# Second-layer sums of a two-layer graph network: gather by tile into a shared ring instead of by step

## What is computed

```
edge_index = stack([src, dst])
x = layernorm(x + layer0(x, edge_index, edge_type_64, ...))

# layer 1
x0_i = leaky(x @ W1 + b1);  x0_j = leaky(x @ W2 + b2)      # slope 0.2
a1 = x0_i @ wa1 + ba1[0];   a2 = x0_j @ wa2 + ba2[0]       # one number per node
row, col = edge_index
att = sigmoid(a1[row] + a2[col])                           # one number per edge
out = segment_sum(att[:, None] * x0_j[col], row, num_segments=12500)
x = layernorm(x + (out + x))
```

## Time and profile before

| | us |
|---|---|
| median of three runs | 7085.9 (7082.45 to 7089.11) |
| span of the profiled execution, first to last instruction | 6353.0 |
| the profiled execution's own device time | not recorded |
| median of the runs less the span of the profile | 732.9 |
| busy: PE / DVE / ACT / POOL | 4654.9 / 4416.1 / 2770.5 / 4352.2 |
| first gather of `attend` starts / last one starts | 4151.36 / 6255.98 |

### The profile page before, as it was taken

How to read it: one execution, slowest core, us unless ns; L and a number is a source line. 1 busy time by engine, 2 the same in 40 slices (tenths; PEclk the granted TensorE clock), 3 DMA queues, 4 the chain that set the end, 5 groups by cost and what they waited for, 6 DMA issues and landing times. The chain is left out here.

```text
span 6353.0 us, 69502 instructions
## 1 busy us (share of the span) xinstructions
PE 4654.9 (73%) x16402; PEld 3170.3 (50%) x16402; DVE 4416.1 (70%) x8998; ACT 2770.5 (44%) x6174; POOL 4352.2 (69%) x4103
## 2 busy tenths in 40 slices
PE   9877878787777777378888879966666666666662
PEld 5565666565666666256666644433333333343331
DVE  8867888888887777867777779945555555555557
ACT  2144444444444444288888847722222222222222
POOL 0067777777777777188787835567777777777773
PEclk9977677777777777599999989977877877767775
DMA  4489999999999999177777723355555665555554
GB/s 149 127 301 338 330 340 340 335 336 335 337 350 341 372 362 367 57 235 223 222 222 222 223 88 102 96 155 158 158 157 157 159 157 157 158 157 158 159 157 135
DMA packets 925700, 1418.46 MB, mean 223 GB/s; under 512 B 93803, under 2 KB 699235, under 8 KB 924985
## 3 DMA queue, kind: packets, MB, share of 16 engines
q1 hardware_dynamic: 705209, 749.70, 37.1%
q0 software_dynamic: 213088, 657.94, 33.4%
q10 hardware_dynamic: 7010, 6.38, 0.3%
HBM read 1140.54 MB, written 273.11 MB: 223 GB/s over the span
## 5 line engine op out<-in xcount | busy, mean ns | idle before, releaser
L653 POOL DMA_INDIRECT s_rows<-kv_rows,other x1664 | 1712.8, 1029 | 507.3 <-issue 471.1
L1401 POOL DMA_INDIRECT t_rows<-xj_rows,other x1664 | 1598.9, 961 | 523.0 <-issue 468.9
L1460 PE MATMUL ps_xsum<-t_rows,t_att 128*128 128x256 f32 x3328 | 1325.8, 550 | 783.2 <-DVE t_att L1426 783.0
L1460 PEld LDWEIGHTS ps_xsum<-t_rows,t_att 128*128 128x128 f32 x3328 | 787.3, 263 | 1321.3 <-DVE t_att L1426 1195.4
L1426 DVE SCALAR_TENSOR_TENSOR t_att<-iota,local,t_att 128x128 f32<-128x128 f32 x1664 | 579.0, 348 | 1037.9 <-ACT t_att L1416 1037.9
L1416 ACT ACTIVATE t_att<-t_att,t_rows 128x128 f32<-128x128 f32 x1664 | 531.2, 389 | 1571.4 <-DMA t_rows<-xj_rows,other 1563.9
L764 PE MATMUL ps_q<-node_tab,hot 128*128 x3328 | 1162.4, 510 | 0.0
L664 ACT ACTIVATE apart<-apart,minus_p 128x1024 bf16<-128x1024 bf16 x416 | 477.6, 1148 | 1221.5 <-DMA apart<-what_rows 1221.4
L1060 PE MATMUL ps_sum<-a_terms,a_hot 128*128 128x260 f32 x3328 | 830.3, 392 | 167.5 <-DVE node_tab L1048 155.0
L762 PE MATMUL ps_rel<-rel,hot 64*128 64x64 f32 x3328 | 583.3, 329 | 495.1 <-ACT hot L669 453.8
L1008 POOL TENSOR_TENSOR a_terms<-a_terms,score 128x1024 f32<-128x1024 f32 x416 | 786.5, 1902 | 193.4 <-DMA a_terms<-v_edges 191.5
(11 more groups left out here) (206 smaller groups left out, 3554.9 us busy)
## 6 DMA issues: line engine op xcount, KB each, us to landing
v_edges<-s_rows SPq DMA_DIRECT2D x416, 512.0 KB, 6.5
a_terms<-v_edges SPq DMA_DIRECT2D x416, 512.0 KB, 4.4
apart<-what_rows SPq DMA_DIRECT2D x416, 256.0 KB, 8.3
t_att<-a_rows SPq DMA_DIRECT2D x416, 256.0 KB, 3.5
s_rows<-kv_rows,other POOLq DMA_INDIRECT x1664, 6.0
t_rows<-xj_rows,other POOLq DMA_INDIRECT x1664, 3.2
kv_rows<-kv_out SPq DMA_DIRECT2D x97, 256.0 KB, 2.0
xj_rows<-n_hx SPq DMA_DIRECT2D x97, 130.0 KB, 2.3
```

Of the source, the lines that this page charges most:

```text
L653: pool.indirect_dma_start(out=rows[g % KV_RING][:, k, :], out_offset=None, in_=t["kv_rows"], in_offset=bass.IndirectOffsetOnAxis(ap=t["oth ...
L1401: pool.indirect_dma_start(out=rows[g % RING][:, k, :], out_offset=None, in_=t["xj_rows"], in_offset=bass.IndirectOffsetOnAxis(ap=t["other1 ...
L1460: nc.tensor.matmul(ps_sum[g % 4][:, k, :], att[g % ATT_RING][:, k, :], rows[g % RING][:, k, 0:D], start=True, stop=True)\
```

## The change

Layer 1's gathers go by tile, not by step. `RING` becomes 32 tiles, one tensor, with 8 `LANDING` semaphores for groups of four tiles. There are `TG` = 391 groups of tiles, 1564 gathers, where there were 1664; a step reads its tile from slot (step - block) mod 32.

- `build_steps(1)`: `other1` is in tile order, made by 13 transposes in place of 25 matmuls. GpSimd also zeroes `places1` and makes two number rows (`step_id`, `tile_base`).
- `attend`: VectorE makes three tables before its loop: `t_slots` (the slot of each step), `t_needs` (for each group of steps, how many groups of tiles must have landed) and, with TensorE, `t_ends` (for each group of tiles, the step that ends its use).
- GpSimd waits for `freed` in place of `summed`. SyncE waits for each group of tiles in turn, counts `landed` up, then waits until the group four behind is summed and counts `freed` up.
- ScalarE takes over the a1 loads from SyncE, five groups ahead (`LEAD`), and reads `t_needs` and `t_slots` into registers; TensorE reads `t_slots` too. Both address `t_rows` by register.
- `softmax_numerators` puts its semaphores into `t["spent"]`, so they are cleared too.

```diff
-RING = 14
+RING = 32
+LANDING = RING // U
+TG = -(-T // U)
+LEAD = 5
...
+def slots_of(nc, eng, slots, g):
+    at = (g % QUARTER) * U
+    return nc.values_load_multi_w_load_instructions(
+        slots[g // QUARTER * 32:g // QUARTER * 32 + 1, at:at + U], engines=[eng.engine], min_val=0, max_val=RING - 1, ...)[1]
...
                 for c in chunks:
+                    if layer and v:
+                        last = nc.tensor.transpose(ps_val[n % BANKS][:, c - chunks[0], :], arrays[v][:, c, :].bitcast(fp32), t["ident"][:, :])
+                        continue
...
         @block.sync
...
             sp.wait_ge(a1_stored, 2 * 16)
-            for g in range(G):
-                if g >= ATT_RING:
-                    sp.wait_ge(summed, (g - ATT_RING + 1) * U)
-                sp.dma_start(att[g % ATT_RING]..., t["a1_rows"][g * U:(g + 1) * U, :]...).then_inc(a1_in[g % ATT_RING], 16)
+            sp.wait_ge(ends_set, 1)
+            for j in range(TG):
+                sp.wait_ge(rows_in[j % LANDING], 16 * U * (j // LANDING + 1))
+                sp.sem_inc(landed, 1)
+                if 0 <= j - 4 < TG - LANDING:
+                    end = sp.value_load(ends[0:1, j - 4:j - 3], min_val=U, max_val=S)
+                    sp.wait_ge(summed, end)
+                    sp.sem_inc(freed, 1)

         @block.gpsimd
         def _(pool):
-            for g in range(G):
-                if g >= RING:
-                    pool.wait_ge(summed, (g - RING + 1) * U)
-                for k in range(U):
-                    pool.indirect_dma_start(out=rows[g % RING][:, k, :], ..., ap=t["other1"][:, g * U + k:g * U + k + 1], axis=0))\
-                        .then_inc(rows_in[g % RING], 16)
+            for j in range(TG):
+                if j >= LANDING:
+                    pool.wait_ge(freed, j - LANDING + 1)
+                for tile in range(j * U, (j + 1) * U):
+                    at = tile % RING * XW
+                    pool.indirect_dma_start(out=rows[:, at:at + XW], ..., ap=t["other1"][:, tile:tile + 1], axis=0))\
+                        .then_inc(rows_in[j % LANDING], 16)

         @block.scalar
...
+            def load_a1(g):
+                if g >= ATT_RING:
+                    act.wait_ge(summed, (g - ATT_RING + 1) * U)
+                act.dma_start(att[g % ATT_RING]..., t["a1_rows"][g * U:(g + 1) * U, :]...).then_inc(a1_in[g % ATT_RING], 16)
...
             for g in range(G):
+                if g + LEAD < G:
+                    load_a1(g + LEAD)
+                at = g % QUARTER
+                need = act.value_load(needs[g // QUARTER * 32:g // QUARTER * 32 + 1, at:at + 1], min_val=1, max_val=TG)
+                slot = slots_of(nc, act, slots, g)
                 act.wait_ge(a1_in[g % ATT_RING], 16 * (g // ATT_RING + 1))
-                act.wait_ge(rows_in[g % RING], 16 * U * (g // RING + 1))
+                act.wait_ge(landed, need)
                 for k in range(U):
                     last = nc.scalar.activation(att[g % ATT_RING][:, k, :], att[g % ATT_RING][:, k, :], ACT.Sigmoid,
-                                                bias=rows[g % RING][:, k, D:D + 1])
+                                                bias=rows[:, bass.ds(slot[k] * XW + D, 1)])
...
             for g in range(G):
+                slot = slots_of(nc, pe, slots, g)
                 for k in range(U):
...
-                    nc.tensor.matmul(ps_sum[g % 4][:, k, :], att[g % ATT_RING][:, k, :], rows[g % RING][:, k, 0:D], ...)
+                    nc.tensor.matmul(ps_sum[g % 4][:, k, :], att[g % ATT_RING][:, k, :], rows[:, bass.ds(slot[k] * XW, D)], ...)
```

More of the change, by code:

```diff
@@ L149, in blocks_of @@
         skip_runtime_bounds_check_because="the merged order of tiles and blocks ends at the last block")[1]
+def slots_of(nc, eng, slots, g):
+    at = (g % QUARTER) * U
+    return nc.values_load_multi_w_load_instructions(
+        slots[g // QUARTER * 32:g // QUARTER * 32 + 1, at:at + U], engines=[eng.engine], min_val=0, max_val=RING - 1,
+        skip_runtime_bounds_check_because="the numbers were cut to the ring's size")[1]
 def gnn_kernel(nc, x, src, dst, edge_type, query, wq, bq, wk, bk, wv, bv, rel_w, wo, bo, gamma, beta,
@@ L194, in gnn_kernel @@
         t["block_hot"] = sb("block_hot", [P, S])
+        t["step_id"], t["tile_base"] = sb("step_id", [P, S // 4], i32), sb("tile_base", [P, C])
+        t["tile_end1"] = sb("tile_end1", [P, C, 2])
         with ExitStack() as middle:
@@ L423, in build_steps @@
         iota_p = sb("iota_p", [P, P])
-        tile_end = sb("tile_end", [P, C, 2])
+        tile_end = t["tile_end1"] if layer else sb("tile_end", [P, C, 2])
         block_row = sb("block_row", [P, C, P])
@@ L476, in _ @@
                 pool.sem_inc(pads_set, 1)
+            else:
+                step(nc.gpsimd.memset(places[:, :], 0))
             step(nc.gpsimd.iota(iota_p[:, :], [[1, P]], base=P, channel_multiplier=0,
@@ L482, in _ @@
             pool.sem_inc(ids_set, 1)
+            if layer:
+                step(nc.gpsimd.iota(t["step_id"][:, :], [[1, S // 4]], base=0, channel_multiplier=S // 4 // 32))
+                step(nc.gpsimd.iota(t["tile_base"][:, :], [[P, C]], base=1, channel_multiplier=0,
+                                    allow_small_or_imprecise_dtypes=True))
         @block.scalar
@@ L788, in sem @@
         def sem(name):
-            return ctx.enter_context(nc.semaphore(name))
+            t["spent"].append(ctx.enter_context(nc.semaphore(name)))
+            return t["spent"][-1]
         W = S * H
@@ L1370, in attend @@
         tab = t["node_tab"]
-        rows = [sb(f"t_rows{u}", [P, U, XW]) for u in range(RING)]
+        rows = sb("t_rows", [P, RING * XW])
+        slots, needs = sb("t_slots", [P, S // 4], i32), sb("t_needs", [P, S // 16], i32)
+        ends_at, ends_diag, ends = sb("t_ends_at", [P, C]), sb("t_ends_diag", [P, C, P // U]), sb("t_ends", [1, C * P // U], i32)
         att = [sb(f"t_att{u}", [P, U, P]) for u in range(ATT_RING)]
@@ L1375, in attend @@
         ps_a1 = ps_sum[3][0:NB, 0, 0:P]
+        ps_ends = ps_sum[2][0:1, 0:2, :].rearrange("p k e -> p (k e)")[:, 0:C * P // U]
         ps_steps = [ps_sum[u][:, :, :].rearrange("p k (two e) -> p (k two) e", e=P) for u in range(2)]
         halves = ((0, 8), (8, C))
-        rows_in, a1_in = [sem(f"t_rows_in{u}") for u in range(RING)], [sem(f"t_a1_in{u}") for u in range(ATT_RING)]
+        rows_in, a1_in = [sem(f"t_rows_in{u}") for u in range(LANDING)], [sem(f"t_a1_in{u}") for u in range(ATT_RING)]
         a1_turned, a1_staged, a1_spread, a1_copied, a1_stored = (sem(f"t_a1_{n}") for n in ("turned", "staged", "spread", "copied", "stored"))
         att_ready, hot_att_ready, summed, added = sem("att_ready"), sem("hot_att_ready"), sem("t_summed"), sem("t_added")
+        landed, freed, table_step = sem("t_landed"), sem("t_freed"), sem("t_table_step")
+        slots_set, needs_set, ends_spread, ends_summed, ends_set = (sem(f"t_{n}") for n in ("slots_set", "needs_set", "ends_spread", "ends_summed", "ends_set"))
         block = ctx.enter_context(nc.Block())
@@ L1388, in _ @@
             sp.wait_ge(a1_stored, 2 * 16)
-            for g in range(G):
-                if g >= ATT_RING:
-                    sp.wait_ge(summed, (g - ATT_RING + 1) * U)
-                sp.dma_start(att[g % ATT_RING][:, :, :].rearrange("p k e -> p (k e)"),
-                             t["a1_rows"][g * U:(g + 1) * U, :].rearrange("k e -> (k e)").partition_broadcast(P)).then_inc(a1_in[g % ATT_RING], 16)
+            sp.wait_ge(ends_set, 1)
[6 more added lines that the diff above has]
+                    sp.sem_inc(freed, 1)
         @block.gpsimd
         def _(pool):
-            for g in range(G):
-                if g >= RING:
-                    pool.wait_ge(summed, (g - RING + 1) * U)
-                for k in range(U):
-                    pool.indirect_dma_start(out=rows[g % RING][:, k, :], out_offset=None, in_=t["xj_rows"],
-                                            in_offset=bass.IndirectOffsetOnAxis(ap=t["other1"][:, g * U + k:g * U + k + 1], axis=0))\
-                        .then_inc(rows_in[g % RING], 16)
+            for j in range(TG):
[3 more added lines that the diff above has]
+                    at = tile % RING * XW
+                    pool.indirect_dma_start(out=rows[:, at:at + XW], out_offset=None, in_=t["xj_rows"],
+                                            in_offset=bass.IndirectOffsetOnAxis(ap=t["other1"][:, tile:tile + 1], axis=0))\
+                        .then_inc(rows_in[j % LANDING], 16)
         @block.scalar
@@ L1411, in _ @@
                 nc.scalar.copy(a1_steps[:, lo:hi, :], ps_steps[n][:, 0:hi - lo, :]).then_inc(a1_copied, 1)
-            for g in range(G):
+            def load_a1(g):
+                if g >= ATT_RING:
+                    act.wait_ge(summed, (g - ATT_RING + 1) * U)
+                act.dma_start(att[g % ATT_RING][:, :, :].rearrange("p k e -> p (k e)"),
```

(30 more changed lines are left out.)

## The result

The changed kernel takes 6954.3 us (median of 4, 6949.19 to 6958.95), the one before on the same chip 7087.5 us (4 runs): -133 us between the medians, which is 0.981 of before. The ratio on record is 0.9826 (95% interval 0.9813 to 0.9839), which is 123 us less; the two don't quite agree, and the gain is 123 to 133 us. The forecast was 6960, -126.6.

What follows compares the result with a forecast made beforehand. GpSimd's 1664 gather issues, 1.2656 us apart, were taken to bound `attend`. Terms -126.6 + 3 - 4 + 1 = -126.6 us took 7085.9 to 6959, said as 6960, range 6938 to 7000.

Steps and rivals of the forecast that it cites:

- part 1: GpSimd's gathers in `attend`: 1664 become 1564, so 100 x 1.2656 = 126.6 us go if the pace stays.
- part 5: The ends: +3 us (0 to +5) after `attend`, -4 (-4 to 0) in `build_steps(1)`, +1 (0 to 1.6) in `aggregate`.
- parts 2, 3: ScalarE, TensorE and VectorE in `attend`: all stay under 4.76 us per group despite new loads and registers; no cost.
- The cover: ScalarE's wait for rows in `attend`, up to 5.26 us per group, hides its added work; 0.3 us spare at the upper end.
- my bound of 0.6: A register load on ScalarE in `attend` takes at most 0.6 us.
- My upper end of 4.5 us: ScalarE's work per group in `attend`, at most: 0.5 DMA, two loads 1.2, six register instructions 1.2, activations 1.6.
- part 4: The shorter ring, 32 gathers ahead for 56, and `freed` passing through SyncE in `attend`: no cost taken.
- 8 us that were to be left: Slack in `attend` between SyncE's freeing of a tile group and GpSimd's gather that needs it.
- 1: Rival: ScalarE or TensorE becomes the bound of `attend` at 4.9 us per group, losing 58 us, 7018; chance 0.09.
- rival 2: ScalarE's a1 loads in `attend` wait for sums and stop activations making later sums: slower, 7186 us; chance 0.05.
- rival 3: GpSimd waits for `freed` so often in `attend` that 1564 gathers take as long as 1664: 7086 us; chance 0.02.
- 4: Rival: time around the span grows with the longer program, a few us to 100, about 7000 us; chance 0.02.

Runs made afterwards that it cites:

- before on 10: The kernel before, profiled again on chip 10 with no edit, twice: 6358.9 us and 6358.0 us.
- changed on 7: The changed kernel, with no edit, beside the kernel before on chip 7: 6212.4 us, ratio 0.9771.
- more loads: The changed kernel with slots read by four one-number loads per group in place of one load of four, on ScalarE and TensorE: 6211.4 us, ratio 0.9771.
- the ring of 16: The changed kernel with a ring of 16 tiles in place of 32, SyncE freeing two groups behind in place of four: 6214.6 us, ratio 0.9775.
- the earlier trace: The profile of the kernel before that the prediction was made from, with a span of 6353.0 us.
- the three chips: The chips of the follow-up runs, numbered 10, 7 and 15, on which the kernel before takes 6356.0 to 6359.5 us.
- the second chip: Chip 7, which ran the changed kernel with no edit (6212.4 us) and the kernel before with a ring of 32 and with registers.
- the third: Chip 15, which ran the one-tensor ring in the kernel before, and the changed kernel with more loads (6211.4 us) and with the ring of 16 (6214.6 us).
- the slow chip: The chip of the first result, without a number on record: the kernel before took 7087.5 us there, the changed kernel 6954.3 us.
- the repeats: Two further profiled runs of the kernel before, with no edit: 6358.9 us (span 6346.7) and 6358.0 us (span 6353.4).

## Why the prediction was right, and where it wasn't

**The cause.** GpSimd's queue is the length of `attend`, and 100 gathers less are 100 intervals less. On chips where profile and time belong together (before on 10, changed on 7), first to last gather goes from 2102.8 us (4146.84 to 6249.63) to 1958.4 (4140.53 to 6098.89). Of these 144.4 us, 126.5 are 100 x 1.2645, as in part 1; the other 18 are 1563 intervals that are 0.0116 shorter. I had bounded the pace at 1.262 to 1.270 us and it came to 1.2529 (1.2549 with more loads and with the ring of 16): that is the one large term outside its bounds, and its cause is open. The bounds themselves were added up loosely: those of the pace and of part 5 give 6950 to 6973, where the prediction says 6945 to 6975.

**ScalarE and TensorE (parts 2, 3).** The cover held. In the changed kernel's trace there a load on ScalarE takes 0.30 us at the median, half my bound of 0.6, and the register instruction ahead of an activation 0.055, where I allowed 0.2; the extra loads moved nothing. My upper end of 4.5 us per group was far too high: ScalarE still waits 3.5 us for `landed` in a group.

```profile
5200.90 0.69 ACT L1466 ACTIVATE t_att<-t_att,t_rows 128x128 f32<-128x128 f32 x2 [3.52 <-SPq L1421]
5201.50 0.68 ACT L1466 ACTIVATE t_att<-t_att,t_rows 128x128 f32<-128x128 f32 x2
5205.64 0.69 ACT L1466 ACTIVATE t_att<-t_att,t_rows 128x128 f32<-128x128 f32 x2 [3.47 <-SPq L1421]
```

The register instructions between activations don't lengthen them either: 0.60 us from pair to pair, as in the 1.28 for four of the earlier trace rows. The 0.6 us that the Trainium skill gives for a `tensor_load` (DMA: Bandwidth & Descriptors, Latency and other measured facts) is twice the record here; the trace decides.

**The ring (part 4).** Right on the three chips that it costs nothing, and too cautious in the slack: of the 8 us that were to be left, the trace on the second chip has 12.3 at the median and 10.1 at least between `freed` and the gather that needs it, and a ring of 16 was enough on the third. On the slow chip the way from a group's first gather to its `freed` is 42.5 us at the median, 27.8 on the second, and GpSimd does wait.

**The ends (part 5).** The last activations in the timeline of the changed kernel on the second chip, which answer to the earlier trace rows:

```profile
6104.71 1.28 ACT L1466 ACTIVATE t_att<-t_att,t_rows 128x128 f32<-128x128 f32 x4 [6.57 <-SPq L1421]
6106.16 1.28 ACT L1466 ACTIVATE t_att<-t_att,t_rows 128x128 f32<-128x128 f32 x4 [0.17 <-issue]
```

Its products for the partner table, by line (busy us, mean ns, idle before), which answer to the earlier trace rows:

```profile
L586 PE MATMUL ps_val<-ident,scratch 128*128 128x128 f32 x13 | 2.1, 273 | 0.0
```

Its timeline at the start of `aggregate`, which answers to the earlier trace rows:

```profile
2697.47 14.85 SPq L1021 DMA_DIRECT2D a_terms<-v_edges  x12
2703.74 9.34 POOL L1032 TENSOR_TENSOR a_terms<-a_terms,score 128x1024 f32<-128x1024 f32 x5 [10.76 <-issue]
```

Two groups follow the last landing, and the time after the last gather's start goes from 97.1 to 100.8 us: +3.7 for a forecast +3. The partner table takes 2.1 us in place of 6.8: -4.7 for -4. From SyncE's first DMA to the first product are 6.27 us, not 4.71: +1.6, the upper bound, for +1; the wait is no longer put down to the DMA, and the trace has 88 clears of a semaphore, 44 ns each and 72 ns apart, from 2697.3 to 2703.6. In before the 66 clears end at 2708.35, 0.1 us ahead of the first product as well: they were the wait, not the DMA that the earlier trace rows puts it down to, and the first DMA hides no part of them. The partner table's -4.7 lies a little outside my -4 to 0. With -144.4 that sums to -143.8; the spans differ by 147.0, and since the two spans of before differ by 6.7 among themselves (6346.7 and 6353.4), the rest can't be assigned.

**The absolute number.** 6960 for 6954.3 came out by a wrong step: "the 732.9 us by which the median exceeds the span I take as unchanged". There is no such time around the span (2 us in every execution with both recorded). What I had was, by all that the repeats show, the sum for one chip and the time of another, on which the program is 11% longer. That 6960 fell 6 us from the measured time is luck: an interval that I priced at 1.2656 us is 1.444 there, so 100 of them are 144 us and not 126.6, and something that I didn't have gave 11 to 21 us of it back, for the measured gain there is 123 to 133.

On the slow chip the changed kernel's gathers are 1.444 us apart ((6841.95 - 4584.89) / 1563). If before's other phases were as long there as the changed kernel's (4584.89 us ahead of the first gather, about 4 more for the partner table and 1.6 less for the clears, 2 us outside the span, and 102 after the last gather's start), its `attend` had 7085.5 - 4587 - 102 = 2396 us for 1663 intervals, 1.441 each. That is an estimate: before has no profile of that chip. By it the pace there is the same before and after, while on the three others it got 1% quicker; so whether ScalarE's slow stretches and the waits for `freed` cost the change something there, and whether a ring of 56 would ride over them better, is open.

That the slowness itself isn't the change's is shown by layer 0, whose code is as before: its gathers are 1.588 us apart there and 1.331 on the second chip. The ratio of the forecast, 0.982, is carried by the gathers that are gone; on the three chips that is shown, on the slow one it is the likeliest reading.

**The rivals.** On the three chips, 1, 2 and 3 are out: ScalarE waits for rows, never for the sums in the middle of the phase, and the pace fell. On the slow one, what ScalarE's stretches cost against before is open (1); its a1 loads did wait for sums, 145.3 us in 39 waits of the middle, so the loop of rival 2 bound in places; and GpSimd's waits for `freed` are rival 3's mechanism, though the whole didn't get slower. 4 is out wherever both are recorded: span and time go together.

## What to carry to other kernels

When one engine issues at a fixed beat and all others wait for it, count its instructions: the gain of removing some is their number times the beat, and work added elsewhere is free as long as it fits into a wait (1.4 us more per group went into 3.5 us of waiting here, and the time stayed). Before summing, hold the profile's span against the timed runs. Here they belong together when they differ by 2 us; 733 us meant two machine conditions, and a sum from one doesn't give the microseconds of the other. An addition whose result nothing reads may not be in the program: look for it in the trace.

## What was not expected of the hardware

- The same program took 7087 us in one place and 6356 to 6359 on three chips. On the slow one the recorded register instructions of ScalarE in the changed kernel take 189 ns on the mean and up to 1393, against 74 and 174 on the second chip. It isn't registers alone: in `attend` the waits on a semaphore, 17 ns each on ScalarE elsewhere, reach 1384 ns there too. Activations and vector operations have nearly the same lengths (392 for 389 ns, 348 for 348), and a matmul's record isn't longer (523 for 536), though the mean granted clock is 0.770 for 0.815. The changed kernel's spans there and on the second chip differ by 748 us: 427 of them lie between the first and last gather of layer 0, 299 between those of `attend`, and only 14 in the 1586 us between. What makes the engines slow in these two phases isn't known.
- A gather of 128 rows costs GpSimd 957 or 946 ns (medians on the three chips) by something in the program that isn't shown: ring size alone, layout alone and the gather's own code don't decide it, since the first two leave it at 957 and the same code of layer 0 has both lengths.
- Whether a row has 2048 bytes (`kv_rows`, layer 0) or 1040 (`xj_rows`), the gather's median is 957 ns in the kernel before, so at these sizes the length doesn't go by the bytes. Layer 0's row on the page of the changed kernel on the second chip (busy us, mean ns, idle before):

```profile
L676 POOL DMA_INDIRECT s_rows<-kv_rows,other x1664 | 1708.2, 1027 | 507.3 <-issue 459.4
```

Its median is 957 too; the mean is higher since some gathers there take up to 2.0 us.
